# Four GNN layers on one core: the first 24 edge groups of layer 0 gathered from x and weighted after summing

## The reference, cut to what matters

```
h = relu(layernorm(x))
L0: x += segment_sum((h @ weight[r])[src], dst) + h_bias + h @ loop_weight    # r = edge type, 16 relations, 64x64 each
L1: x += concat(h, segment_sum(h[src], dst)) @ W.T + b
L2: x += segment_mean(relu(concat(h[src], h[dst], attr) @ W1 + b1) @ W2 + b2, dst) + h @ Wn + bn
L3: x += concat(h, segment_sum(concat(h[src], attr) @ W1 + b1, dst)) @ W2 + b2
```

## Time and profile before

| | us |
|---|---|
| median of 3 runs | 5246.6 |
| the profiled execution | 5244.34 |
| its span, first to last instruction | 5242.5 |
| POOL busy | 3689.3 (70%), 3892 instructions |
| PE busy | 3842.8 (73%) |
| DVE busy | 2367.4 (45%) |
| ACT busy | 1975.8 (38%) |
| setup and first_nodes, until the first gather of layer 0 | 247.7 |
| layer 0, first static gather to last | 247.7 to 2196.4 |
| layer 1, from its first gather to the first gather of layer 2 | 2263.9 to 2800.1 |

### The profile page before, as it was taken

The page is one execution under the profiler, slowest core; times in us unless marked ns, Lnnn a source line. Parts: engine busy times, 40 slices in busy tenths (PEclk is TensorE's granted clock), DMA queues, the critical chain, the costliest instruction groups (busy, mean ns, idle before and its releaser), DMA issues. The chain is left out here.

```text
span 5242.5 us, 72102 instructions
## 1 busy us (share of the span) xinstructions
PE 3842.8 (73%) x23400; PEld 2715.2 (52%) x23401; DVE 2367.4 (45%) x6319; ACT 1975.8 (38%) x3506; POOL 3689.3 (70%) x3892
## 2 busy tenths in 40 slices
PE   5757767777777777679985666767777767777897
PEld 3346656555444444435544555555565556664444
DVE  7679866555545555433434222323333333333222
ACT  4513445455555556401112333333333344441000
POOL 3377777777777777767724777777777777776774
PEclk8855556556655566689997999999999999998998
DMA  7712333333333333378862222323333333336886
GB/s 245 293 36 63 104 89 102 90 105 103 103 104 104 104 106 107 92 231 279 267 194 70 79 80 79 83 80 83 83 83 82 83 83 86 82 86 188 278 277 196
DMA packets 484150, 665.96 MB, mean 127 GB/s; under 512 B 136237, under 2 KB 334184, under 8 KB 475603
## 3 DMA queue, kind: packets, MB, share of 16 engines
q1 hardware_dynamic: 292961, 451.27, 25.0%
q0 software_dynamic: 122848, 181.25, 14.7%
q10 hardware_dynamic: 67986, 28.96, 2.1%
HBM read 478.95 MB, written 187.16 MB: 127 GB/s over the span
## 5 line engine op out<-in xcount | busy, mean ns | idle before, releaser
L1249 POOL DMA_INDIRECT layer_msg<-snd_table,idx_src x1536 | 1456.7, 948 | 596.3 <-issue 464.2
L1249 POOL DMA_INDIRECT layer_msg<-rel_table,idx_rel x1536 | 1475.9, 961 | 487.2 <-issue 458.7
L2041 PE MATMUL layer_sum_ps<-layer_sel,layer_msg 128*128 128x128 f32 (+13 forms) x6912 | 1040.2, 300 | 1031.7 <-DVE layer_hidden_acc L1678 541.5
L2041 PEld LDWEIGHTS layer_sum_ps<-layer_sel,layer_msg 128*97 128x97 f32 (+2 forms) x6912 | 943.8, 217 | 1221.4 <-issue 1166.8
L1477 ACT CAST layer_strip<-layer_unit_ps 128x700 fp8e4<-128x700 f32 (+4 forms) x1035 | 865.8, 883 | 911.8 <-PE layer_unit_ps L2082 787.7
L2082 PE MATMUL layer_unit_ps<-layer_frame_hot,layer_low_hot 128*128 128x200 bf16 (+6 forms) x4500 | 857.1, 360 | 151.1 <-ACT layer_strip L1477 86.9
L1666 DVE TENSOR_TENSOR layer_msg<-layer_pre_ps,layer_msg 128x512 f32<-128x512 f32 x392 | 271.0, 691 | 1275.2 <-DMA layer_msg<-snd_table,idx_src 1198.2
L2101 PE MATMUL layer_panel_ps<-layer_piece,layer_pairs 128*128 128x504 fp8e4 (+3 forms) x3136 | 701.8, 379 | 26.7 <-DMA layer_piece<-counts 26.7
L1249 POOL DMA_INDIRECT layer_msg<-h_table,idx_src x576 | 553.1, 960 | 228.0 <-issue 169.2
L2082 PEld LDWEIGHTS layer_unit_ps<-layer_frame_hot,layer_low_hot 128*128 128x128 bf16 x4500 | 496.1, 144 | 408.9 <-ACT layer_strip L1477 267.0
L1747 DVE TENSOR_SCALAR layer_frame_hot<-count_iota,frame_key 128x392 bf16<-128x392 f16 (+6 forms) x2250 | 588.9, 330 | 0.0
(11 more groups left out here) (257 smaller groups left out, 3269.3 us busy)
## 6 DMA issues: line engine op xcount, KB each, us to landing
layer_piece<-counts SPq DMA_DIRECT2D x48, 1575.0 KB
layer_attr<-in_edge_attr_dram SPq DMA_DIRECT2D x790, 64.0 KB
rel_table<-first_rows SPq DMA_DIRECT2D x98, 512.0 KB, 4.6
counts<-layer_strip SPq DMA_DIRECT2D x32, 1543.5 KB
layer_piece<-counts SPq DMA_DIRECT2D x24, 1600.0 KB
layer_piece<-counts SPq DMA_DIRECT2D x18, 1562.5 KB
layer_rcv<-rcv_table SPq DMA_DIRECT2D x396, 64.0 KB, 1.8
counts<-layer_strip SPq DMA_DIRECT2D x16, 1568.0 KB
```

The costliest lines, as they stand in the source:

```text
L1249: nc.gpsimd.indirect_dma_start(msg[g][:, u, 0:2 * D if dense else width], None, of, bass.IndirectOffsetOnAxis(ap=idx[:, at:at + 1], axis=0 ...
L2041: last = nc.tensor.matmul(sum_ps[g % 2][0:rows, 0:span], msg[g][:, u, 0:rows], sel[j][:, u, 0:span], start=u == 0, stop=u == TILES - 1)
```

## The change

1. Groups 0 to 23 (`EARLY`) leave the gathers of layer 0: its loop starts at group 24 (`FIRST` = 3), so that it issues 1440 static gathers instead of 1536. Their rows are gathered from the input x itself (`early_x`, 96 indirect DMAs of 128 rows of 256 bytes) by POOL in first_nodes, whose other work on POOL is reordered around them: the copy to `ht_ac` is gone, the 18 gathers of groups come in a row, and so do the 18 of lists.
2. In layer 0, steps 0 to 23 also handle one early group each: DVE normalises its 512 rows (`make_early`, 8 instructions, with one square root on ACT), and makes a 0/1 matrix over (node, relation); PE sums (`sum_early`), and DVE adds the sum to `by_rel` (64 nodes times 16 relations). After the last, 16 matmuls apply the relation matrices (`weigh_early`), and `finish_early` adds the result to `acc`.
3. Counting shares its buffers with this, so the unpacking starts at step 27 and the counting at step 38 of 360 steps; it ends at step 356.
4. In first_nodes h is split into two fp16 halves and w0 into three bf16 parts, so that `split` is one DVE instruction. It is still three matmuls for a product.
5. In setup, DVE and PE wait for the loads themselves, and `everything` is gone. A list for the key (16*offset + type) of the early groups is added: one DVE instruction and 4 transposes and 2 ACT copies, and three small DVE instructions.
6. In layer 1, own products and table products of a block are 7 matmuls of 320 columns instead of 7 of 64 and 7 of 256.

```diff
+EARLY, EARLY_NODES = 24, 64
...
-                sp.wait_ge(loaded, 16 * len(loads))
-                sp.sem_inc(everything, 1)
...
-                dve.wait_ge(everything, 1)
...
+                dve.wait_ge(loaded, 16 * LOADS)
...
+                gather_x(range(AHEAD))
+                pool.wait_ge(groups_found, 1)
...
+                gather_x(range(AHEAD, EARLY * TILES))
+                pool.wait_ge(places_found, 1)
+                pool.wait_ge(table_stored, 16)
...
-                    link(nc.vector.tensor_tensor(rest[D:P, :], ht_ps[0:D, 0:BLK], ht_ab[s][0:D, :],
-                                                 ALU.subtract))
-                    link(nc.vector.tensor_copy(ht_ab[s][D:P, :], rest[D:P, :]))
-                    link(nc.vector.tensor_tensor(ht_ac[s][D:P, :], rest[D:P, :], ht_ab[s][D:P, :],
-                                                 ALU.subtract))
+                    link(nc.vector.scalar_tensor_tensor(out=ht[s][D:P, :], in0=ht_ps[0:D, 0:BLK], scalar=HIGH,
+                                                        in1=ht[s][0:D, :], op0=ALU.mult, op1=ALU.subtract))
...
-    FIRST = DENSE_1 // PER if dense else 0
+    FIRST = DENSE_1 // PER if dense else EARLY // PER if build else 0
...
-            CHUNK_EVERY, BEGIN, END = 2, 12, NG - 4
-            chunk_at = {1 + CHUNK_EVERY * m: m for m in range(len(CHUNKS))}
+            CHUNK_EVERY, BEGIN, END = 2, EARLY + 14, NG - 4
+            CHUNK_FROM = EARLY + 3
...
+                    norm_steps(nc, link, early_x[:, e, :, :], early_mean[:, :], early_rstd[:, :], early_xc, early_sq)
+                    dve.sem_inc(early_var, 1)
+                    if e >= 2:
+                        dve.wait_ge(early_summed, e - 1)
+                    nc.vector.tensor_tensor(
+                        early_sel[e % 2][:, :, :],
+                        rel_key[:, e * TILES:(e + 1) * TILES].unsqueeze(2).to_broadcast([P, TILES, P]),
+                        window_iota.unsqueeze(1).to_broadcast([P, TILES, P]), ALU.is_equal).then_inc(early_ready, 1)
+                    dve.wait_ge(early_std, e + 1)
+                    link(nc.vector.reciprocal(early_rstd[:, :], early_rstd[:, :]))
+                    nc.vector.scalar_tensor_tensor(
+                        out=early_msg[e % 2][:, :, 0:D], in0=early_xc[:, :, :], scalar=0.0,
+                        in1=early_rstd[:, :].unsqueeze(2).to_broadcast([P, TILES, D]), op0=ALU.max,
+                        op1=ALU.mult).then_inc(early_ready, 1)
...
+                    nc.vector.tensor_tensor(to, to, early_ps[e % 2], ALU.add).then_inc(early_added, 1)
...
                         for k in range(KW):
                             act.wait_ge(rows_ready, m * KW + k + 1)
-                            nc.scalar.copy(rows[:, :, k * H:(k + 1) * H],
-                                           row_ps[k % 2].rearrange("p (t f) -> p t f", t=2)
-                                           ).then_inc(rows_copied, 1)
+                            nc.scalar.copy(rows[:, k, :], row_ps[k % 2]).then_inc(rows_copied, 1)
...
+                    if q < EARLY:
+                                sum_early(q)
...
+                        for part in range(3):
+                            last = nc.tensor.matmul(to, ht[s][:, nodes], w0_parts[:, part, c0:c1],
+                                                    start=part == 0, stop=part == 2)
```

More of the change, by code:

```diff
@@ L616, in _ @@
                     turned_lists = turn_ps[n % 4][:, :].rearrange("p (u g) -> p u g", u=TILES)
-                    groups = min(P, G - c * P)
-                    if c == 0:
+                    groups = EARLY if to is rel_key else min(P, G - c * P)
+                    if c == 0 and to is not rel_key:
                         nc.scalar.activation(
@@ L819, in _ @@
+                for c in range(LIST_CH):
+                    nc.gpsimd.indirect_dma_start(
+                        lists[:, c, :], None, list_table,
+                        bass.IndirectOffsetOnAxis(ap=place_i[:, c:c + 1], axis=0)).then_inc(lists_in, 16)
             @block.vector
@@ L1090, in layer_phase @@
         msg = [sb(f"msg{g}", [P, TILES, 2 * D], F16) if dense else
-               sb(f"msg{g}", [P, TILES, P if layer == 0 else width]) for g in range(PER)]
+               sb(f"msg{g}", [P, TILES, width if layer else DEG + 1]) for g in range(PER)]
         sel = [sb(f"sel{j}", [P, TILES, P], F16 if dense else F32) for j in range(SLOTS)]
@@ L1124, in layer_phase @@
         ht_ps = ps("ht_ps") if mlp else post_ps
-        row_ps = [ps(f"row_ps{i}")[:, 0:2 * H] for i in range(2)] if nxt == 2 else None
+        row_ps = [ps(f"row_ps{i}")[:, 0:D + 2 * H] for i in range(2)] if nxt == 2 else None
         out_w = D + 1 if nxt == 2 else D
@@ L2128, in node_part @@
                         pe.wait_ge(ht_ready, m * 2 + 3)
+                    if part == 9 and nxt != 2:
                         for k in range(KW):
```

261 lines of the change are left out of this document (194 added, 67 removed).

## The result

The changed kernel takes **5119.1 us** (median of 4 runs, 5116.3 to 5127.7), the kernel before, run beside it, 5247.1 us (4 runs, 5243.5 to 5252.6): a ratio of 0.9757, 95% interval 0.9744 to 0.9770. Forecast were 5117 us and a range of 5098 to 5150. So between the traces there are 116.6 us, between the medians 128; further down a second trace of nearly the same kernel, with an execution of 5116.1 us, shows where the difference is.

A forecast was written before the change was run, and what follows sets the result against it. POOL's row of gathers was taken to bound layer 0. From the profiled 5244.3 us, -16 (setup and first_nodes), -101 (layer 0) and -12 (layer 1) gave 5115, plus 2.3 for the median: 5117 us, range 5098 to 5150.

The forecast's parts named there:

- POOL's row of gathers bounds layer 0: Layer 0 is as long as POOL's gathers; 96 fewer at 1.249 us each give -119.9 us, stalls counted apart.
- Setup: Before first_nodes: DVE no longer waits for the semaphore behind the packed store, -3 us, bounds 0 and -4.
- first_nodes: POOL ends at 227.5 us, first gather of layer 0 at 231 instead of 247.66; -16 us together with setup.
- The early steps: Layer 0, steps 0 to 23: DVE's step takes 4.95 us against POOL's 5.0, so its distance stays at 16 us.
- The port: Layer 0, early steps: two-input SBUF instructions on DVE slow gathers by 0.19 us per us, +6 us, bounds 0 and +12.
- Counting in fewer steps: Layer 0: counting units spread over 318 instead of 368 groups bring new POOL stalls, +13 us, bounds +8 and +35.
- Layer 1: Merged products shorten PE's path by 0.8 us in 12 blocks and 1 us in each of the last two: -12 us.
- (a): Rival, layer 0's early steps: DVE can't keep the pace, time 5131 to 5155 us; chance 0.09.
- (b): Rival, first_nodes: gathers take 1.45 us each or wait for DMA, 26 us later, 5143 us; chance 0.06.
- (c): Rival: the port lock holds POOL for whole DVE instructions in early steps and first_nodes, +53, 5170 us; chance 0.03.
- (d): Rival, layer 0: counting doesn't shrink with fewer steps and consumers set the time, 5349 us, slower; chance 0.03.
- (e): Rival, layer 0: POOL isn't the limit, so only layer 1 and first_nodes gain, 5219 us; chance 0.03.

The follow-up runs named there:

- experiment 2: Merged products of layer 1 alone, put into the kernel before: 5235.9 us against 5245.6, ratio 0.9980.
- experiment 3: Kernel before with only the fp16 halves and shorter setup wait, no x rows gathered in first_nodes: 5220.3 us, ratio 0.9949.
- experiment 4: Changed kernel with 16 early groups instead of 24: 5140.5 us.
- experiment 10: Kernel before with another cost table for the counting units: 5238.7 us against 5248.2, ratio 0.9978.
- experiment 1: The changed kernel measured again without an edit: 5120.6 us, ratio 0.9754 to the kernel before.
- experiment 5: Changed kernel with 33 instead of 28 gathers of x rows ahead of the wait for the group search: 5118.2 us.
- experiment 6: Changed kernel with another cost table for the counting units, putting fewer units into the first steps: 5106.9 us, ratio 0.9726 to the kernel before.
- experiment 7: Changed kernel with five more two-input DVE instructions in each of the 24 early steps: 5137.8 us, ratio 0.9785 to the kernel before.
- experiment 8: Changed kernel with both 33 gathers ahead of the group search and the other counting cost table: 5099.9 us, ratio 0.9714 to the kernel before.
- experiment 9: Changed kernel where POOL, ending first_nodes, also waits for the list gathers to land and clears a scratch tile as mark: 5123.8 us.

## Why the forecast was right, and where it was not

**POOL's row of gathers bounds layer 0: right.** 96 gathers less, and the layer is shorter by 101.7 us. Of the 119.9 us, about 13 went into new stalls by the starts of the gathers (forecast +13), 15.1 by the view of waits, and 6.7 into slower gathers: 1440 x (965.5 - 960.9) ns (forecast +6).

**Setup: right**, 2.8 us for 3.

**first_nodes: POOL's and PE's ends right, the step behind them wrong.** (The stores were done 4 us sooner than I had them, at 224.0 for 228.) "The first gather of layer 0 comes about 2.4 us behind the last end, as now behind the last store's landing" was the step that failed. Behind the last store's landing it is 1.8 us, in each of the five traces in which SP is last (before, experiments 2, 3, 4 and 10). When POOL is last, 9.3 to 9.75 us follow its last gather or the mark behind it (after, experiments 1 and 5 to 9), 7.3 us more than I put in: -9.6 instead of -16 for both phases. I took the end of POOL's last gather for POOL's end, but its DRAIN ends 6.8 to 9.0 us later in every trace. That of before had it, 6.8 us behind the last gather and hidden beside the stores; with these and 1.5 us of crossing I would have put the first gather at 235.8 instead of 231.

**The early steps: the size was wrong, without consequence.** 3.91 us, because the starts of neighbouring short instructions overlap and I had added durations and gaps. The distance from a group's last gather to its sum fell from 18.9 us at group 0 to 3.5 at group 14 instead of staying at 16. It was worth nothing, as POOL doesn't run faster for it; experiment 7 shows what the other side would have cost. Nor did my 16 us at step 38 harm the next term. By the starts in both traces the distance was 3.3 us before counting began before and 3.4 after, so that the two stretches could be compared as they stood: it rose from 3.4 at step 40 to 54.0 at step 54, stalls included, where I had a rise of 51.

**The port: the size was wrong.** I took 0.19 us per us of two-input instructions from one chunk of unpacking and got +6 for the early steps. They lost 1.8 us (what the gathers took above 944 ns each), and with 32 us more of such instructions in 96 us nothing was added. The loss beside unpacking is real (3.1 us in those 12 steps after, 4.0 before), but two inputs in SBUF aren't enough to cause it; what does stays open. That layer 0's gathers are 6.7 us slower all the same comes from later steps: 6.5 and 8.7 us were lost in steps 100 to 199 and 200 to 299, instead of 5.1 and 5.2. There is more counting beside each, but no experiment isolates it. The Trainium skill, page SBUF — State Buffer, section "SBUF: two separate sides", has the other fully blocked for the whole instruction, for DVE instructions with two SBUF inputs against a GpSimd operation that reads SBUF; I had left that condition out. Whether the reading of a gather's indices falls under it that section doesn't say. The same page of the Trainium skill, section "Who interferes with whom", tells of a probe in which tensor_tensor did not stall DMAs issued by GpSimd; experiment 7 agrees, with 967 ns for 966.

**Counting in fewer steps: right**, in size and place (steps 44 to 75), and shown by experiments 6 and 10: spreading the units by DVE's cost takes the stalls away. What I had as PE's waits "half as long" was wrong: 345.9 us became 278.9, with the longest 5.2.

```profile
PE layer_sum_ps L2182 <- DMA layer_msg<-rel_table,idx_rel: 278.9, 132, 5.2
...
1100.00:1500.00 400.00, 286.41 (x1623) 194.82 (x1623) 244.89 (x760) 249.49 (x351) 304.00 (x316) 0.70 0.36 110
```

In the same 400 us before PE ran 1485 matmuls in 285.05 us at a granted clock of 0.62: 9% more of them now take the same time, as the clock is 0.70. I had counted TensorE's time as fixed.

**Layer 1: the sum near, the place wrong.** -12 was -7.3 in the trace of after, -10.4 in two others, -9.7 alone. Of it 9.6 us were to come from "-0.8 us in 12 blocks on PE's path", and the blocks beside the static gathers gave 0.4, although the products of each were 0.95 us shorter. The third line of the earlier trace rows shows PE at 98.45 of 100 us there, and I stopped reading; in the same row POOL has 76.22 us in 79 instructions, and 79 x 0.30 us of issue make it 99.9. Two engines were full, and the one that isn't shortened kept the time. The other 2 us, for the last two blocks, were too small: five blocks stand behind the last static gather, where PE is on the path. Three of them saved 0.95 us each, and the last two, which ran at a granted clock of 0.50 for most of their products, 2.0 and 2.9. I had the full clock of the earlier trace rows for all.

**The rivals.** (a) DVE stays ahead: refuted, and experiment 7 at 6.26 us a step cost 17 us, where (a) had +14 for 6 us. (b) a gather in first_nodes took 1.03 us plus issue on the mean of the 96, not 1.45 in all, but a part of it is real: 8.5 us over 0.944 in all. (c) refuted by experiment 7. (d) and (e) refuted by the result. The forecast of 5117 for 5119 owes something to luck: 6 us too much gain before layer 0 and 2 to 5 in layer 1 stand against a base, profiled executions, that moves by several us from run to run.

**Where the gain is from.** It isn't that an early group is cheaper; its four gathers cost POOL no less in first_nodes, 1.03 us and 0.30 of issue each. They lie there in time that POOL had free. Experiment 3 shows the limit: without them that phase ends 16.8 us earlier. With 24 groups POOL is full and last, with 16 it isn't (experiment 4). By an estimate from that trace, 25.4 us of waiting at 5.3 us a group, it is full at about 21 groups; each further one costs there what it saves in layer 0, which wasn't measured by itself.

## What to carry to other kernels

Work moved to an engine's idle time pays until that engine is the last one of the phase that takes it in; look for that point, and for what leaving the phase costs when another engine is last. An engine is full when its busy time and its issue gaps make the stretch, so count the gaps before you call another engine at 98% the bound. When work is spread over fewer steps, spread it by the cost on the engine that has none to spare: here the table was worth about a tenth of the change.

## What the runs showed of the hardware

- POOL's DRAIN at the end of first_nodes ends 6.8 to 9.0 us behind POOL's last work there (12 traces), also when that work has landed (experiment 9); the next phase's first gather follows 1.5 us behind that when nothing else is waited for. When POOL is last that makes 9.3 to 9.75 us; when SP's stores are, the first gather comes 1.8 us behind the last landing.
- 32 us of DVE instructions with two SBUF inputs of 128x256, added beside 75 gathers, changed a gather's mean time on POOL by 1 ns.
- The same 14 matmuls of 97x64 took 1.67 us at a granted clock of 1.00 and 3.25 at 0.50 (layer 1 of the kernel before).
- In layer 0 PE's clock was granted higher (0.70 for 0.62 between 1100 and 1500 us) when more matmuls fell into the same time.
- Executions of one kernel differ by up to 21 us here (5116.1 to 5137.1), part of it in a gather's median of 944 or 947 ns: over some 3800 gathers 3 ns are 11 us.
